# A graph kernel's node pass shared over three spread stages instead of two, and one DVE step moved

## The chip, the core and the metric

The kernel runs on one core of one Trainium2 chip. The core has five engines that take their own instruction streams and meet at semaphores: PE (TensorE, matrix products; its weight loads are shown apart as PEld), DVE (VectorE), ACT (ScalarE), POOL (GpSimd; here it issues the gathers) and SP (SyncE; here it issues the plain DMAs). The metric is the device time of one execution in microseconds (us), as the median of several runs. A lower time is better.

## The reference, cut to what matters

50,000 nodes with 64 features (N, D), 25,000 edges sorted by destination. Two layers, each on a layer norm with a ReLU: four GAT attention layers in a row, and one crystal-graph convolution. Cut:

```
h  = relu(layernorm(x))
for i in range(4):                              # L = 4 attention layers
    fs    = (h @ Ws[i]).reshape(N, 4, 64)
    e     = leaky_relu(el[src] + er[dst])
    alpha = softmax of e over the edges of one destination (self loops too)
    h     = segment_sum(alpha * fs[src], dst).sum(heads) + bias
x1 = x + h + h_bias                             # "x1": every node, all 50,000
h  = relu(layernorm(x1))
t  = batch_norm(concat(h[src], h[dst], edge_attr) @ W_full)
x  = x1 + softplus(h + batch_norm(segment_sum(sigmoid(t1) * softplus(t2), dst)))
```

Most nodes are no destination of any edge. For those the four attention layers reduce to one fixed 64x64 product on relu(layernorm(x)). The kernel computes that product for all nodes in a **node pass** (98 groups of 512 nodes), which needs nothing of the attention layers, and writes rows of x1 to a table; rows for destinations come from the edge side.

## The kernel before

Edges are padded to 196 tiles of 128, taken as G = 49 groups of 4 tiles (512 edges). Each attention layer l is a row of stages with barriers between them: softmax_weights (some 20 us), messages(l), and for l = 0, 1, 2 spread(l). The semaphores of a layer are cleared behind its stages. After the last layer come the convolution, its batch norms and the output.

**spread(l)** carries the sums of a destination back along its edges and fetches each edge's source row. It has 49 edge groups. What is done per edge group k, by engine:

- POOL: four indirect gathers (L930), 4 buffers of groups deep: it waits for the scan of group k-4 and else runs freely.
- SP: a load of the mask row keep_next (L940).
- PE: weights (L974), one 64x512 product, and dst_side (L981), four 128x72 products.
- DVE: end, the masking (ended, L1015), back, a reversed scan (h_new, L1022) that follows the scan of the group before, and combine (L1030 to L1032), which needs the gathered rows of the group and dst_side.
- ACT: finish, a copy of the scan into wide (L1079).

In spread(0) and spread(1) (`with_nodes = l < 2`) the same loop also carries one node group per edge group, 49 in each, so that all 98 are done; spread(2) has none. The node work of a group:

- SP: load_nodes (L946), and save_nodes, two stores (L952, L954). The load waits for x1_ready of the group four back.
- DVE: n_sum L1036, n_center L1041, n_variance L1046, n_normalize L1051, n_finish L1057 (adds nodes to bank 5, writes x1_out, raises x1_ready).
- ACT: n_squares L1084, n_scales L1088 and L1090, n_take L1095 (copies the transposes out).
- PE: n_transposes (L989), n_outs (L996), four 128x64 products into bank 5. n_outs waits for n_take of its group and x1_ready of the group before, since bank 5 is one buffer.

The order on each engine is written by hand: `pipelined(eng, stages)` runs i = 0 to 52 and, in each turn i, calls every (lag, fn) of the list with k = i - lag, if 0 <= k < 49. So the list's order is the engine's order within a turn. A **turn** below is one i. Before, DVE's list is normalize(3), end(1), back(1), combine(3), variance(2), sum(1), center(1), finish(4), the lag in brackets; PE's is outs(4), weights(0), transposes(3), dst_side(2).

Of the kernel before, what the change touches and what calls it, by code (L numbers as in the profile page):

```python
# [28 lines left out]
P = 128  # L29
D = 64  # L30
H = 4
L = 4
# [6 lines left out]
G = TILES // TPG  # L39
# [7 lines left out]
NODE_T2 = 4  # L47
GN2 = NODE_T2 * P
# [4 lines left out]
AHEAD = 4  # L53
# [38 lines left out]
def build(nc, x, src, dst, edge_attr, Ws, attn_l, attn_r, gat_bias, h_bias, W_full, b_full,  # L92
# [5 lines left out]
    LAST_P2 = (N - (2 * G - 1) * GN2) // NODE_T2  # L98
# [17 lines left out]
    def mem(stack, name, shape, dt=F32):  # L116
        return stack.enter_context(nc.sbuf_tensor(name, shape, dt))
# [3 lines left out]
    def sem(stack, name):  # L121
        signals.append(nc.alloc_semaphore(name=name))
        return signals[-1]
# [17 lines left out]
    with top:  # L141
# [742 lines left out]
        def spread(l):  # L884
# [2 lines left out]

            with ExitStack() as st:
                SLOTS = 4
                uses = [(G - s + SLOTS - 1) // SLOTS for s in range(SLOTS)]  # L890
                with_nodes = l < 2
                if with_nodes:
                    nodes = mem(st, f"nodes_{l}", [P, SLOTS, NODE_T2, D])
                    x1_out = mem(st, f"x1_out_{l}", [P, 2, NODE_T2, 2 * D])
                    n_norm = mem(st, f"n_norm_{l}", [P, SLOTS, NODE_T2, D + 1])
                    n_square = mem(st, f"n_square_{l}", [P, NODE_T2, D])
                    n_norm_t = mem(st, f"n_norm_t_{l}", [D + 1, GN2])
                    n_stat = mem(st, f"n_stat_{l}", [P, SLOTS, 3, NODE_T2])
                    n_logs = mem(st, f"n_logs_{l}", [P, NODE_T2])
                    nodes_in = [sem(st, f"nodes_in_{l}_{s}") for s in range(SLOTS)]  # L900
                    x1_saved = [sem(st, f"x1_saved_{l}_{s}") for s in range(2)]
                    ones_set = sem(st, f"ones_set_{l}")
                    n_summed, n_centered, n_squared, n_summed2, n_logged, n_rstd, n_normed, n_in_psum, n_t_ready, n_out, x1_ready = [
                        sem(st, f"n_{name}_{l}") for name in ("summed", "centered", "squared", "summed2", "logged", "rstd", "normed",
                                                             "in_psum", "t_ready", "out", "x1_ready")]
# [29 lines left out]
                @block.sync  # L935
                def _(sp):
                    def load(k, g, s, turn):
                        sp.wait_ge(spread_out, at(k, back=2))
                        sp.sem_inc(sp_paced, 1)
                        sp.dma_start(keep[:, s % 2], lanes(keep_row[bass.ds(g * GE + 1, GE)], D)).then_inc(keep_in[s], 16)  # L940

                    def load_nodes(k, g, s, turn):
                        used = LAST_P2 if isinstance(k, int) and k == G - 1 and l == 1 else P
                        sp.wait_ge(x1_ready, at(k, back=4))
                        sp.sem_inc(sp_paced, 1)
                        sp.dma_start(nodes[0:used, s], x[bass.ds((k + l * G) * GN2, used * NODE_T2)].rearrange("(p j) f -> p j f", j=NODE_T2)).then_inc(nodes_in[s], 16)  # L946

                    def save_nodes(k, g, s, turn):
                        used = LAST_P2 if isinstance(k, int) and k == G - 1 and l == 1 else P
                        sp.wait_ge(x1_ready, at(k))  # L950
                        sp.sem_inc(sp_paced, 1)
                        sp.dma_start(tables[L - 1][bass.ds((k + l * G) * GN2, used * NODE_T2)].rearrange("(p j) f -> p j f", j=NODE_T2),  # L952
                                     x1_out[0:used, s % 2, :, 0:D]).then_inc(x1_saved[s % 2], 16)
                        sp.dma_start(node_rows[bass.ds((k + l * G) * GN2, used * NODE_T2)].rearrange("(p j) f -> p j f", j=NODE_T2),  # L954
                                     x1_out[0:used, s % 2]).then_inc(x1_saved[s % 2], 16)

                    if with_nodes:
                        sp.wait_ge(ones_set, 3)
                        for s in range(2):
                            sp.sem_inc(x1_saved[s], 16)  # L960
                        pipelined(sp, ((0, load), (4, save_nodes), (0, load_nodes)), down=True, slots=SLOTS)
                        for s in range(2):
                            sp.wait_ge(x1_saved[s], 32 * (uses[s] + uses[s + 2]) + 16)
                    else:
                        pipelined(sp, ((0, load),), down=True, slots=SLOTS)

                @block.tensor
                def _(t_):
# [30 lines left out]
                    if with_nodes:  # L999
                        for signal in (n_in_psum, n_out):  # L1000
                            t_.sem_inc(signal, AHEAD)
                        pipelined(t_, ((4, n_outs), (0, weights), (3, n_transposes), (2, dst_side)), down=True, slots=SLOTS)
                    else:
                        pipelined(t_, ((0, weights), (2, dst_side)), down=True, slots=SLOTS)

                @block.vector
                def _(v):
# [51 lines left out]
                    if with_nodes:  # L1059
                        for signal in (n_summed, n_centered, n_summed2, n_normed, x1_ready):  # L1060
                            v.sem_inc(signal, AHEAD)
                        v.memset(n_norm[:], 1.0).then_inc(ones_set, 1)
                        v.memset(nodes[:], 0.0).then_inc(ones_set, 1)
                        v.memset(x1_out[:, :, :, D:2 * D], 0.0).then_inc(ones_set, 1)
                        v.wait_ge(ones_set, 3)
                        pipelined(v, ((3, n_normalize), (1, end), (1, back), (3, combine), (2, n_variance), (1, n_sum), (1, n_center),
                                      (4, n_finish)), down=True, slots=SLOTS)
                    else:
                        pipelined(v, ((1, end), (1, back), (3, combine)), down=True, slots=SLOTS)

                @block.scalar
                def _(s_):
# [24 lines left out]
                    if with_nodes:  # L1097
                        for signal in (n_squared, n_logged, n_rstd, n_t_ready):
                            s_.sem_inc(signal, AHEAD)
                        pipelined(s_, ((1, finish), (3, n_take), (2, n_scales), (1, n_squares)), down=True, slots=SLOTS)  # L1100
                    else:
                        pipelined(s_, ((1, finish),), down=True, slots=SLOTS)

        def attention_step(l):
            with ExitStack() as st:
# [675 lines left out]
```

## Time and profile before

| | us |
|---|---|
| median of 3 runs | 3240.72 |
| lowest, highest run | 3231.77, 3241.5 |
| the profiled execution, its own time | 3232.58 |
| its span, first to last instruction | 3230.8 |
| mean granted TensorE clock over the span | 0.818 of 2.4 GHz |

Busy over the span: PE 2319.8 us (72%), DVE 2235.8 (69%), POOL 1427.3 (44%), ACT 1248.5 (39%). No engine is the bound of the whole; each stage has a limit of its own. The three spreads are found in the timeline by POOL's gathers of L930: spread(0) begins at 818 us, spread(1) at 1341, spread(2) at 1869; each ends where DVE's first step of the next softmax (L649) starts.

A timeline row reads: start us, duration us, engine, line, operation, output <- input, count, and in brackets the engine's idle time ahead of it and what released it.

### The profile page before, as it was taken

To read this page: it belongs to the slowest core of one execution; us is meant where nothing else is said; L and a number is where in the kernel's file an instruction comes from. 1 tells how busy PE (TensorE), PEld (TensorE's weight loads), DVE (VectorE), ACT (ScalarE), POOL (GpSimd) and SP (SyncE) were. 2 spreads that over 40 slices of the span, in tenths; PEclk is the share of its full clock that TensorE was granted. 3 is DMA by queue.
4 is the path that set the end of the run, shared out by engine and by line. 5 is a ranking of instruction groups with operands and counts; after the bars stand their busy time and mean duration, and the time that the engine had idled before them with its cause. 6 is when DMAs were issued, how large, how long until landed. Compare 5 with 4: busy or idle time off the path is not lost. (4 is left out here: it accounts for less than half of the span.)

```text
span 3230.8 us, 38240 instructions
## 1 busy us (share of the span) xinstructions
PE 2319.8 (72%) x10796; PEld 1499.2 (46%) x10796; DVE 2235.8 (69%) x3888; ACT 1248.5 (39%) x2599; POOL 1427.3 (44%) x1389
## 2 busy tenths in 40 slices
PE   1998888399788689889859977739977772110575
PEld 1766665255565445466635533325533331000565
DVE  4766664677777677677767744458889986664698
ACT  0333323244333234333324411114445556663587
POOL 5777774000677200377500067720057763777000
PEclk9999999999767689866759965559989985555898
DMA  2333332011444301255411111102233321222464
GB/s 60 105 108 99 94 100 78 15 46 46 101 124 123 85 32 46 62 124 125 118 30 47 46 37 34 34 13 79 78 74 72 72 63 30 63 71 67 138 202 139
DMA packets 310382, 248.80 MB, mean 77 GB/s; under 512 B 149840, under 2 KB 258639, under 8 KB 310154
## 3 DMA queue, kind: packets, MB, share of 16 engines
q1 hardware_dynamic: 266270, 197.56, 20.1%
q0 software_dynamic: 43904, 48.80, 8.3%
q8 instruction: 90, 1.47, 0.2%
q14 instruction: 118, 0.97, 0.1%
HBM read 125.76 MB, written 118.06 MB: 75 GB/s over the span
## 5 line engine op out<-in xcount | busy, mean ns | idle before, releaser
L930 POOL DMA_INDIRECT edge<-table,row_of_source x588 | 589.3, 1002 | 963.6 <-POOLq L753 778.8
L871 PE MATMUL banks<-scaled_t,w_heads 128*64 128x512 f32 x784 | 380.3, 607 | 0.0
L815 DVE TENSOR_TENSOR_SCAN wide<-keep,wide,banks 64x512 f32<-64x512 uint8 x196 | 249.5, 1273 | 187.4 <-issue 162.6
L1238 POOL DMA_INDIRECT edge<-table,row_of_x x196 | 227.3, 1160 | 303.4 <-POOLq L131 242.2
L981 PEld LDWEIGHTS banks<-w_edge_full,wide 128*128 128x128 f32 x1176 | 219.9, 279 | 146.6 <-issue 139.5
L849 ACT ACTIVATE ring<-wide 128x512 f32<-128x512 f32 x196 | 123.6, 630 | 425.1 <-DVE wide L815 425.1
L981 PE MATMUL banks<-w_edge_full,wide 128*128 128x72 f32 x1176 | 227.5, 360 | 70.5 <-DVE self_logit L1032 69.7
L1497 POOL DMA_INDIRECT node_rows<-rows_conv,scatter_row x196 | 218.9, 1117 | 118.3 <-ACT rows_conv L1535 68.0
L878 PEld LDWEIGHTS banks<-w_row,ring 128*128 128x128 f32 x1568 | 189.7, 191 | 160.9 <-issue 149.3
L974 PE MATMUL banks<-wide,w_row 128*64 128x512 f32 x294 | 250.6, 953 | 16.2 <-DVEq L1009 9.9
L1079 ACT ACTIVATE wide<-h_new 64x512 f32<-64x512 f32 x147 | 92.6, 630 | 435.4 <-DVE h_new L1022 435.4
L808 DVE TENSOR_TENSOR scaled<-edge,alpha 128x1024 f32<-128x1024 f32 x196 | 236.7, 1209 | 3.7 <-PE banks L863 3.7
L190 POOL DMA_INDIRECT edge<-in_x_dram,src_row x196 | 194.2, 991 | 81.4 <-issue 57.9
L190 POOL DMA_INDIRECT got<-in_x_dram,dst_row x196 | 194.4, 992 | 59.7 <-issue 59.1
L878 PE MATMUL banks<-w_row,ring 128*128 128x68 f32 (+1 forms) x1568 | 217.1, 281 | 4.6 <-ACT ring L849 4.6
L863 PE MATMUL banks<-ident,scaled 128*128 128x128 f32 x1568 | 210.3, 279 | 11.4 <-DVE scaled L808 11.4
L1611 PE MATMUL banks<-ident,last_sum 64*128 64x64 f32 x196 | 32.3, 318 | 247.8 <-ACT rows_conv L1535 192.6
L587 PE MATMUL banks<-w_chain,norm_t 64*128 64x204 f32 x392 | 204.8, 625 | 2.5 <-ACT self_logit L565 2.5
L996 PE MATMUL banks<-w_node,n_norm_t 65*128 65x64 f32 x784 | 144.8, 346 | 73.5 <-DVE x_out L1057 69.5
L863 PEld LDWEIGHTS banks<-ident,scaled 128*128 128x128 f32 x1568 | 184.1, 150 | 16.3 <-DVE scaled L808 12.8
L1022 DVE TENSOR_TENSOR_SCAN h_new<-keep_next,h_new,ended 64x512 f32<-64x512 uint8 x147 | 187.9, 1278 | 5.2
L996 PEld LDWEIGHTS banks<-w_node,n_norm_t 65*128 65x128 f32 x784 | 134.1, 257 | 80.5 <-issue 64.9
(300 smaller groups left out, 4530.6 us busy)
## 6 DMA issues: line engine op xcount, KB each, us to landing
node_rows<-x_out SPq DMA_DIRECT2D x97, 256.0 KB
wide<-node_rows SPq DMA_DIRECT2D x48, 512.0 KB, 3.6
table<-chain_rows SPq DMA_DIRECT2D x147, 136.0 KB, 2.2
table<-rows SPq DMA_DIRECT2D x147, 136.0 KB, 2.3
nodes<-in_x_dram SPq DMA_DIRECT2D x97, 128.0 KB, 2.9
table<-x_out SPq DMA_DIRECT2D x97, 128.0 KB
out_dram<-n_soft SPq DMA_DIRECT2D x48, 256.0 KB, 2.1
sources<-src_pad SPq DMA_DIRECT2D x49, 196.0 KB
```

The costliest lines, as they stand in the source:

```text
L190: pool.indirect_dma_start(out=to, out_offset=None, in_=x, in_offset=bass.IndirectOffsetOnAxis(ap=rows[:, tile:tile + 1], axis=0),).then_in ...
L808: v.tensor_tensor(scaled[:, s], edge[:, tiles, 0:D].unsqueeze(2).broadcast_to([P, TPG, H, D]), inner(alpha[:, tiles], [P, TPG, H, D]), ALU ...
L815: v.tensor_tensor_scan(out=wide[0:D, bass.ds(g * GE + 1, GE)], data0=keep[:, s], data1=bank[2 + s][0:D], initial=wide[0:D, bass.ds(g * GE, ...
L863: last = t_.transpose(bank[6 * s + pair][:, t * P:(t + 1) * P], scaled[:, s, t, 2 * pair:2 * pair + 2].rearrange("p h f -> p (h f)"), iden ...
L871: last = t_.matmul(bank[2 + s][0:D], w_heads[:, l, pair], scaled_t[:, s, pair], start=pair == 0, stop=pair == 1)
L878: last = t_.matmul(bank[4 + s][:, t * width:(t + 1) * width], ring[:, s, t * P:(t + 1) * P], w_row[:, l, 0:width], start=True, stop=True)
L930: pool.indirect_dma_start(out=edge[:, at_tile], out_offset=None, in_=tables[l], in_offset=bass.IndirectOffsetOnAxis(ap=row_of_source[:, at ...
L974: t_.matmul(bank[s % 2][0:D], w_row[:, l, 0:D], wide[:, bass.ds(g * GE + 1, GE)], start=True, stop=True).then_inc(through, 1)
L981: last = t_.matmul(bank[2 + s % 2][:, t * EDGE_W:(t + 1) * EDGE_W], here, w_edge_full[:, l + 1], start=True, stop=True)
L996: last = t_.matmul(bank[5][:, j * D:(j + 1) * D], n_norm_t[:, j * P:(j + 1) * P], w_node[:], start=True, stop=True)
L1238: pool.indirect_dma_start(out=edge[:, tile, 0:D], out_offset=None, in_=tables[l], in_offset=bass.IndirectOffsetOnAxis(ap=row_of_x1[:, tile ...
L1497: pool.indirect_dma_start(out=node_rows, out_offset=bass.IndirectOffsetOnAxis(ap=scatter_row[:, tile:tile + 1], axis=0), in_=rows[:, s, t] ...
```

## The change

The 98 node groups are shared over the three spreads: 32, 33 and 33 (2·49·l // 3 is the first). The node stages of a spread are called only for k < 32 or 33, through a wrapper `some`; the edge groups stay 49 in each. spread(2) now has the node buffers, semaphores, three memsets and the end's wait on the stores that the other two had. On DVE, n_finish moves from the end of a turn to behind end, ahead of back.

```diff
-                with_nodes = l < 2
-                if with_nodes:
-                    nodes = mem(st, f"nodes_{l}", [P, SLOTS, NODE_T2, D])
+                first_group = 2 * G * l // (L - 1)
+                groups = 2 * G * (l + 1) // (L - 1) - first_group
+
+                def some(fn):
+                    return lambda k, g, s, turn: fn(k, g, s, turn) if k < groups else None
+
+                nodes = mem(st, f"nodes_{l}", [P, SLOTS, NODE_T2, D])
...
-                        sp.dma_start(nodes[0:used, s], x[bass.ds((k + l * G) * GN2, used * NODE_T2)].rearrange("(p j) f -> p j f", j=NODE_T2)).then_inc(nodes_in[s], 16)
+                        sp.dma_start(nodes[0:used, s], x[bass.ds((k + first_group) * GN2, used * NODE_T2)].rearrange("(p j) f -> p j f", j=NODE_T2)).then_inc(nodes_in[s], 16)
...
+                    pipelined(sp, ((0, load), (4, some(save_nodes)), (0, some(load_nodes))), down=True, slots=SLOTS)
+                    for s in range(2):
+                        sp.wait_ge(x1_saved[s], 32 * ((groups - s + 1) // 2) + 16)
...
-                        pipelined(t_, ((4, n_outs), (0, weights), (3, n_transposes), (2, dst_side)), down=True, slots=SLOTS)
-                    else:
-                        pipelined(t_, ((0, weights), (2, dst_side)), down=True, slots=SLOTS)
+                    pipelined(t_, ((4, some(n_outs)), (0, weights), (3, some(n_transposes)), (2, dst_side)), down=True, slots=SLOTS)
...
-                        pipelined(v, ((3, n_normalize), (1, end), (1, back), (3, combine), (2, n_variance), (1, n_sum), (1, n_center),
-                                      (4, n_finish)), down=True, slots=SLOTS)
-                    else:
-                        pipelined(v, ((1, end), (1, back), (3, combine)), down=True, slots=SLOTS)
+                    pipelined(v, ((3, some(n_normalize)), (1, end), (4, some(n_finish)), (1, back), (3, combine), (2, some(n_variance)),
+                                  (1, some(n_sum)), (1, some(n_center))), down=True, slots=SLOTS)
...
-                        pipelined(s_, ((1, finish), (3, n_take), (2, n_scales), (1, n_squares)), down=True, slots=SLOTS)
-                    else:
-                        pipelined(s_, ((1, finish),), down=True, slots=SLOTS)
+                    pipelined(s_, ((1, finish), (3, some(n_take)), (2, some(n_scales)), (1, some(n_squares))), down=True, slots=SLOTS)
```

DVE in spread(0), one turn in the run of full turns. Before:

```order
L1051 SCALAR_TENSOR_TENSOR n_norm_0<-n_norm_0,n_stat_0 128x4x64
L1015 SCALAR_TENSOR_TENSOR ended_0<-keep_next_0,banks 64x512
L1022 SCALAR_TENSOR_TENSOR h_new_0<-keep_next_0,h_new_0,ended_0 64x512
L1030 TENSOR_TENSOR edge<-edge,banks 128x4x64
L1031 TENSOR_TENSOR edge<-edge,banks 128x4x4
L1032 TENSOR_SCALAR self_logit<-banks 128x16
L1046 TENSOR_REDUCE n_stat_0<-n_square_0 128x4
L1036 TENSOR_REDUCE n_stat_0<-nodes_0 128x4
L1041 SCALAR_TENSOR_TENSOR n_norm_0<-n_stat_0,nodes_0 128x4x64
L1057 TENSOR_TENSOR x1_out_0<-banks,nodes_0 128x4x64
```

The change, the last turn that still has n_normalize, the last with n_finish, and the first with neither (lines are three or so less, since the code above them is shorter):

```order
L1048 SCALAR_TENSOR_TENSOR n_norm_0<-n_norm_0,n_stat_0 128x4x64
L1012 SCALAR_TENSOR_TENSOR ended_0<-keep_next_0,banks 64x512
L1054 TENSOR_TENSOR x1_out_0<-banks,nodes_0 128x4x64
L1019 SCALAR_TENSOR_TENSOR h_new_0<-keep_next_0,h_new_0,ended_0 64x512
L1027 TENSOR_TENSOR edge<-edge,banks 128x4x64
L1028 TENSOR_TENSOR edge<-edge,banks 128x4x4
L1029 TENSOR_SCALAR self_logit<-banks 128x16
L1012 SCALAR_TENSOR_TENSOR ended_0<-keep_next_0,banks 64x512
L1054 TENSOR_TENSOR x1_out_0<-banks,nodes_0 128x4x64
L1019 SCALAR_TENSOR_TENSOR h_new_0<-keep_next_0,h_new_0,ended_0 64x512
```

The step x1_out now stands between ended and the scan h_new, and after it only the edge steps are left.

PE in spread(0) where the node groups stop. Before, at the same place, the four kinds go on to the stage's end:

```order
L974 MATMUL banks<-wide,w_row 64x512
L989 MATMUL banks<-ident,n_norm_0 65x128 x4
L981 MATMUL banks<-w_edge_full,wide 128x72 x4
L996 MATMUL banks<-w_node,n_norm_t_0 128x64 x4
L974 MATMUL banks<-wide,w_row 64x512
L989 MATMUL banks<-ident,n_norm_0 65x128 x4
```

The change:

```order
L981 MATMUL banks<-w_edge_full,wide 128x72 x4
L996 MATMUL banks<-w_node,n_norm_t_0 128x64 x4
L974 MATMUL banks<-wide,w_row 64x512
L981 MATMUL banks<-w_edge_full,wide 128x72 x4
L974 MATMUL banks<-wide,w_row 64x512
L981 MATMUL banks<-w_edge_full,wide 128x72 x4
```

The last turns of the stage hold weights and dst_side alone, as all turns of spread(2) did before.

## Rows read from the trace of the kernel before

**Rows 1.** Windows, the three spreads: stretch, length, busy and instructions by engine, clock, DMA.

```profile
818.00:1105.00 287.00, 242.47 (x1078) 170.93 (x1078) 209.67 (x493) 97.80 (x246) 200.60 (x196) 0.71 0.48 118
1341.00:1630.00 289.00, 252.43 (x1078) 178.68 (x1078) 209.27 (x492) 96.83 (x246) 195.49 (x196) 0.68 0.48 118
1868.00:2124.00 256.00, 177.27 (x490) 95.95 (x490) 120.21 (x246) 32.13 (x50) 193.26 (x196) 0.55 0.19 33
```

**Rows 2.** Groups by line, POOL alone, spread(0), (1), (2): busy, mean ns, idle before.

```profile
L930 POOL DMA_INDIRECT edge<-table,row_of_source x196 | 200.6, 1023 | 309.2 <-POOLq L753 249.8 <-issue 59.4
...
L930 POOL DMA_INDIRECT edge<-table,row_of_source x196 | 195.5, 997 | 328.8 <-POOLq L753 262.9 <-issue 57.6 <-DVE h_new L1022 8.3
...
L930 POOL DMA_INDIRECT edge<-table,row_of_source x196 | 193.3, 986 | 325.6 <-POOLq L753 266.2 <-issue 59.4
```

**Rows 3.** Timeline: first gather of each spread, last combine, first step behind it.

```profile
818.21 0.94 POOL L930 DMA_INDIRECT edge<-table,row_of_source  x1 [249.77 <-POOLq L753]
...
1112.56 0.97 DVE L649 TENSOR_TENSOR edge<-edge,const_logit 128x784 f32<-128x784 f32 x1 [7.50 <-PEq L131]
...
1341.13 0.94 POOL L930 DMA_INDIRECT edge<-table,row_of_source  x1 [262.89 <-POOLq L753]
...
1638.54 0.98 DVE L649 TENSOR_TENSOR edge<-edge,const_logit 128x784 f32<-128x784 f32 x1 [8.11 <-PEq L131]
...
1868.66 0.94 POOL L930 DMA_INDIRECT edge<-table,row_of_source  x1 [266.15 <-POOLq L753]
...
2122.88 0.42 DVE L1030 TENSOR_TENSOR edge<-edge,banks 128x256 f32<-128x256 f32 x1 [4.38 <-DMA edge<-table,row_of_source]
...
2131.80 0.97 DVE L649 TENSOR_TENSOR edge<-edge,const_logit 128x784 f32<-128x784 f32 x1 [8.33 <-PEq L131]
```

**Rows 4.** Timeline, POOL: the first gather of edge group k = 32 in each spread.

```profile
986.87 0.94 POOL L930 DMA_INDIRECT edge<-table,row_of_source  x1 [0.30 <-issue]
...
1507.74 1.35 POOL L930 DMA_INDIRECT edge<-table,row_of_source  x1 [0.31 <-issue]
...
2034.35 0.94 POOL L930 DMA_INDIRECT edge<-table,row_of_source  x1 [0.31 <-issue]
```

**Rows 5.** Timeline, DVE in spread(0): the scans of groups 3, 32 and 48.

```profile
835.24 1.28 DVE L1022 TENSOR_TENSOR_SCAN h_new<-keep_next,h_new,ended 64x512 f32<-64x512 uint8 x1
...
1000.26 1.28 DVE L1022 TENSOR_TENSOR_SCAN h_new<-keep_next,h_new,ended 64x512 f32<-64x512 uint8 x1
...
1090.84 1.28 DVE L1022 TENSOR_TENSOR_SCAN h_new<-keep_next,h_new,ended 64x512 f32<-64x512 uint8 x1
```

**Rows 6.** Timeline, PE in spread(1): one turn at the low clock.

```profile
1489.66 1.90 PE L996 MATMUL banks<-w_node,n_norm_t 65*128 65x64 f32 x8
1491.50 1.97 PE L974 MATMUL banks<-wide,w_row 128*64 128x512 f32 x2
1493.39 1.12 PE L989 MATMUL banks<-ident,n_norm 128*65 128x128 f32 x4
1494.31 1.82 PE L981 MATMUL banks<-w_edge_full,wide 128*128 128x72 f32 x8
1495.92 1.47 PE L996 MATMUL banks<-w_node,n_norm_t 65*128 65x64 f32 x6
```

**Rows 7.** Timeline in spread(0), a turn at the full clock: scan, ACT's copy, n_take.

```profile
1069.48 1.27 DVE L1022 TENSOR_TENSOR_SCAN h_new<-keep_next,h_new,ended 64x512 f32<-64x512 uint8 x1
...
1070.88 0.63 ACT L1079 ACTIVATE wide<-h_new 64x512 f32<-64x512 f32 x1 [1.92 <-DVE h_new L1022]
...
1071.53 0.59 ACT L1095 ACTIVATE n_norm_t<-banks 65x512 f32<-65x512 f32 x1
```

**Rows 8.** Waits in spread(0): engine and line, released by, us in total, times, longest.

```profile
DVE n_stat L1036 <- DMA nodes<-in_x_dram: 48.8, 41, 2.3
```

**Rows 9.** Timeline, DVE at the start of spread(2): scans of groups 0 and 3.

```profile
1871.34 1.28 DVE L1022 TENSOR_TENSOR_SCAN h_new<-keep_next,h_new,ended 64x512 f32<-64x512 uint8 x1
...
1878.19 1.28 DVE L1022 TENSOR_TENSOR_SCAN h_new<-keep_next,h_new,ended 64x512 f32<-64x512 uint8 x1
```

More of the change, by code:

```diff
@@ new lines, in spread @@
+                n_norm_t = mem(st, f"n_norm_t_{l}", [D + 1, GN2])
+                n_stat = mem(st, f"n_stat_{l}", [P, SLOTS, 3, NODE_T2])
+                n_logs = mem(st, f"n_logs_{l}", [P, NODE_T2])
+                nodes_in = [sem(st, f"nodes_in_{l}_{s}") for s in range(SLOTS)]
+                x1_saved = [sem(st, f"x1_saved_{l}_{s}") for s in range(2)]
+                ones_set = sem(st, f"ones_set_{l}")
+                n_summed, n_centered, n_squared, n_summed2, n_logged, n_rstd, n_normed, n_in_psum, n_t_ready, n_out, x1_ready = [
+                    sem(st, f"n_{name}_{l}") for name in ("summed", "centered", "squared", "summed2", "logged", "rstd", "normed",
+                                                         "in_psum", "t_ready", "out", "x1_ready")]
@@ L953, in save_nodes @@
                                      x1_out[0:used, s % 2, :, 0:D]).then_inc(x1_saved[s % 2], 16)
-                        sp.dma_start(node_rows[bass.ds((k + l * G) * GN2, used * NODE_T2)].rearrange("(p j) f -> p j f", j=NODE_T2),
+                        sp.dma_start(node_rows[bass.ds((k + first_group) * GN2, used * NODE_T2)].rearrange("(p j) f -> p j f", j=NODE_T2),
                                      x1_out[0:used, s % 2]).then_inc(x1_saved[s % 2], 16)
[L957 to L963, printed above, removed]
-                    else:
-                        pipelined(sp, ((0, load),), down=True, slots=SLOTS)
+                    sp.wait_ge(ones_set, 3)
@@ L967, in _ @@
+                    for s in range(2):
+                        sp.sem_inc(x1_saved[s], 16)
+                    pipelined(sp, ((0, load), (4, some(save_nodes)), (0, some(load_nodes))), down=True, slots=SLOTS)
+                    for s in range(2):
+                        sp.wait_ge(x1_saved[s], 32 * ((groups - s + 1) // 2) + 16)
                 @block.tensor
@@ L997, in n_outs @@
                         last.then_inc(n_out, 1)
-                    if with_nodes:
-                        for signal in (n_in_psum, n_out):
-                            t_.sem_inc(signal, AHEAD)
-                        pipelined(t_, ((4, n_outs), (0, weights), (3, n_transposes), (2, dst_side)), down=True, slots=SLOTS)
-                    else:
-                        pipelined(t_, ((0, weights), (2, dst_side)), down=True, slots=SLOTS)
+                    for signal in (n_in_psum, n_out):
+                        t_.sem_inc(signal, AHEAD)
+                    pipelined(t_, ((4, some(n_outs)), (0, weights), (3, some(n_transposes)), (2, dst_side)), down=True, slots=SLOTS)
                 @block.vector
@@ L1057, in n_finish @@
                         v.tensor_tensor(x1_out[:, s % 2, :, 0:D], bank[5][:, 0:NODE_T2 * D].rearrange("p (j f) -> p j f", f=D), nodes[:, s], ALU.add).then_inc(x1_ready, 1)
[L1059 to L1065, printed above, removed]
[L1066 to L1069 removed]
+                    for signal in (n_summed, n_centered, n_summed2, n_normed, x1_ready):
+                        v.sem_inc(signal, AHEAD)
+                    v.memset(n_norm[:], 1.0).then_inc(ones_set, 1)
+                    v.memset(nodes[:], 0.0).then_inc(ones_set, 1)
+                    v.memset(x1_out[:, :, :, D:2 * D], 0.0).then_inc(ones_set, 1)
+                    v.wait_ge(ones_set, 3)
+                    pipelined(v, ((3, some(n_normalize)), (1, end), (4, some(n_finish)), (1, back), (3, combine), (2, some(n_variance)),
+                                  (1, some(n_sum)), (1, some(n_center))), down=True, slots=SLOTS)
                 @block.scalar
```

28 lines of the change are left out of this document (8 added, 20 removed).

## The prediction

> **What bounds the kernel now.** The change touches only the three spreads, so I read the windows of those stretches first. The two with nodes keep PE and DVE well filled over 287 and 289 us; the one without has PE at 177 and DVE at 120 of 256 us [rows 1]. POOL's busy time is nearly the same in all three, 200.6, 195.5 and 193.3 us [rows 2]. The second view is POOL's group by line: its idle time inside a stage is 0.3 us between gathers ("issue", 59.4 us) and, in spread(1) only, 8.3 us behind the scan. So its gathers take 260.0, 261.4 and 252.7 us from first start to last end.
>
> The third view is the timeline at the stages' edges [rows 3]. From the first gather to the first step of the next softmax it is 1112.56 - 818.21 = 294.35 us, 1638.54 - 1341.13 = 297.41 us, and 2131.80 - 1868.66 = 263.14 us: 854.9 us in all. In spread(2) POOL sets the end: its last combine waits for the gather, 1.5 us after POOL's last end (1868.66 + 252.7 = 2121.4, combine at 2122.88), and the softmax starts 10.45 us behind POOL's end. In spread(0) POOL is done 34 us ahead of the stage's end, at 1078.2: there PE and DVE are last. Their pace is (1090.84 - 835.24) / 45 = 5.68 us a turn [rows 5], while POOL's is 260.0 / 49 = 5.31. The gap of some 0.4 us a turn piles up over 49 turns, and a tail of node turns stands behind it.
>
> What makes 5.68: the granted clock in spread(0) is 0.71, a mixture of 1.2 and 2.4 GHz [rows 1]. A turn at the low clock is 6.26 us (1495.92 - 1489.66), of which PE is busy all through [rows 6]: n_outs 1.84, weights 1.89, transposes 0.92, dst_side 1.61, start to start. At the full clock it is shorter and DVE waits for the nodes' load, 48.8 us in spread(0) [rows 8], since the load waits for n_finish at the end of a turn.
>
> **The change part by part.** *Edge groups without nodes.* 17 groups of spread(0) and 16 each of spread(1) and (2) now have none. Such a turn at the low clock costs PE 1.89 + 1.61 = 3.50 us. At the start of spread(2), at the full clock, three turns took 1878.19 - 1871.34 = 6.85, or 2.28 each [rows 9]. POOL wants 5.1 to 5.3. So behind the last node group PE and DVE gain 1.6 us or more a turn on POOL. Do they catch up? I take the worst mixture that the rows show: the old pace as far as group 32, then the low clock throughout. Scan 32 stands at 1000.26 - 818.21 = 182.1 us after the first gather. Two more full turns and one without transposes: 182.1 + 12.5 + 5.3 = 199.9 for scan 35. Thirteen turns of 3.50: 245.4 for scan 48; two more turns and the scan's 1.3: combine 48 could start at 253.7. POOL lets it start at some 255.7 + 1.5 = 257.2 (next step). POOL ends last, by 3.5 us, and by more with any turn at the full clock. What is late next in all three spreads is thus POOL.
>
> *POOL's own time.* It slows a little beside node work. Its first 32 groups took 986.87 - 818.21 = 168.7 us in spread(0), 1507.74 - 1341.13 = 166.6 in spread(1) and 2034.35 - 1868.66 = 165.7 in spread(2), where no nodes were [rows 3, 4]. The remaining 17 groups, without nodes, took 2121.4 - 2034.35 = 87.0. I add 87.0 to each node part: 255.7, 253.6, and for spread(2) the mean of the two node parts, 167.6 + 87.0 = 254.6. POOL also waits for the scan four groups back: group 39 would start near 205, scan 35 ends at 201.2 even in the slow case above, and from there scans run ahead. No term for that.
>
> *The end of a stage.* 10.45 us from POOL's end to the next softmax, as in spread(2). Its stores, formerly behind the last node group, are then long done.
>
> *spread(2)* gets three memsets (they stood ahead of the first turn in the other two, beside POOL's first gathers), the node loads and stores on SP's queue, and more semaphores to clear. Memsets and queue are hidden: POOL waits for nothing of them in its first four groups, and DVE then has the slack above. The clearing does not show in rows; spread(0), with its node semaphores, took 7.50 us behind DVE's last step where spread(2) took 8.33 [rows 3]. I take 0; the ends are 0 and 1 us.
>
> *n_finish behind the masking.* Per turn 0 instructions more. It lets the load start some 3 us earlier (scan, combine, variance, sum, center stood before it) and so should remove most of the 48.8 us of rows 8 at the full clock, and PE's next n_outs comes free earlier. In exchange the scan waits for n_out. The loop that this closes is scan start to ACT's copy 1.40, copy to n_take 0.65, n_take 0.59 [rows 7], n_outs 1.84 at the low clock [rows 6], n_finish 0.42 (its neighbours' length): 4.90 us, below the 6.26 of PE. So no turn gets longer, and turns at the full clock may get down towards POOL's 5.2. Under POOL that is slack: worth 0 in the sum.
>
> **Sum.** Spread(0): 255.7 + 10.45 = 266.1, from 294.35: -28.2. Spread(1): 253.6 + 10.45 = 264.1, from 297.41: -33.3. Spread(2): 254.6 + 10.45 = 265.1, from 263.14: +2.0. Together -59.5 us on the profiled execution's own 3232.58, hence 3173. That execution lies near the lowest of the runs; the three runs and it have a mean of 3236.6. From there: 3177. I give **3177**.
> Bounds of the unknown terms: POOL as quick in all as in spread(2), 3 x 263.14 = 789.4, is -65.5; POOL at spread(0)'s 260.0 over all 49 groups, and 1 us of clearing, is 3 x 270.5 + 1 = 812.3, or -42.6. With the runs' own 3231.8 to 3241.5 that is 3166 to 3199.
>
> **On the clock, the Trainium skill.** The low clock's rows are PE-bound turns; spread(2), whose PE had least work, was granted 0.55 [rows 1]. The Trainium skill says in "TensorE: Matmul & The Clock Gate", section "What's actually happening", that the half-rate state is the default and PE's activity lifts it. By this rule the thinned turns and, in balance with POOL, the node turns would go at the lower rate; the rows of spread(2) agree for the thinned ones.
>
> **Rivals.**
> 1. *PE stays at the low clock through the node turns* as well, because it is no longer behind and so pauses. For it: 0.55 in spread(2) [rows 1]. Against it: at 6.26 PE has no pause, and this very state gave way to the full clock time and again in spreads (0) and (1). Time: scan 3 at 17.0, scan 32 at 17.0 + 29 x 6.26 = 198.6, scan 35 at 216.4, scan 48 at 261.9, combine 48 at 270.2, the softmax 8.9 after it: 279.1 for each spread, 837.3 in all, -17.6 us, so 3219.
> 2. *Slower than before: n_finish's wait holds the scan in a longer loop.* One place: DVE between masking and scan. If PE, in its fixed order, put weights (1.97) between n_take and n_outs, the loop would be 4.90 + 1.97 = 6.87 us a turn at the low clock. A spread is 17.0 + 31 p + 5.3 + 45.5 + 8.3 + 8.9 for a turn of p; it passes 285.0 (854.9 / 3) from p = 6.45. At 6.87 it is 298.0, 894 in all, +39 us, so 3276. Against it: PE's order has n_outs first, and the loop has 1.36 us to spare.
> 3. *The change doesn't do what it says*: spreads (0) and (1) stay as long because the thinned turns don't catch up. If they ran at POOL's 5.16 from scan 35 on: 199.9 + 15 x 5.16 + 1.3 + 8.9 = 287.5 in each, 862.5, +8 us: 3244. Against it: 2.28 a turn in rows 9, and nothing in a thinned turn waits for more than its own gather.
>
> **How the numbers follow.** POOL-bound spreads, my forecast: 0.83. Rival 1 or something between it and the forecast: 0.10. Rival 2: 0.03. Rival 3: 0.04, split evenly between no change and slower. The range takes the forecast's bounds and reaches a little towards rival 1: **3162 to 3205**. A measurement of this kernel tells apart about 0.3%, some 10 us. Faster by more than that: 0.93. Within: 0.02. Slower: 0.05.
>
> **What would show it.** Right: in every spread the last combine waits for the gather's DMA, as in spread(2) before, and the first gather to the softmax is 263 to 268 us three times; POOL has no wait behind the scan; scan 48 of spread(0) stands near 245 after the first gather or earlier, not 273. The wait of n_sum for the nodes' load falls clearly. PE's clock is lower behind group 33 than before it. Wrong: a last combine that waits for dst_side or the scan; POOL waits behind h_new in tens of us; waits at n_finish for n_outs near 1 us in most turns, with turns over 6.3; a gather mean well above 1023 ns; or messages stages that change their length, which the sum takes as fixed.

## The result, and the profile after

The changed kernel takes **3187.18 us** (median of 4 runs, 3185.08 to 3191.02) beside 3236.24 us for the kernel before (4 runs, 3229.4 to 3241.5). The ratio is 0.985, 95% interval [0.983, 0.987]: 1.5% faster, some 49 us. The forecast was 3177, from 3162 to 3205. Its direction and its range held; the gain was 10 to 15 us smaller than the sum.

The profiled execution took 3188.4 us (span 3186.6). The windows of its three spreads answer to [rows 1]; the columns are the same:

```profile
818.00:1077.00 259.00, 223.54 (x874) 149.42 (x874) 176.43 (x407) 74.44 (x178) 197.29 (x196) 0.63 0.43 98
1316.00:1576.00 260.00, 212.75 (x886) 142.15 (x886) 177.75 (x411) 75.62 (x182) 199.83 (x196) 0.67 0.43 100
1816.00:2076.00 260.00, 215.62 (x886) 142.56 (x886) 177.77 (x410) 76.05 (x182) 199.81 (x196) 0.66 0.43 99
```

The three are alike now, PE at 213 to 224 us and DVE at 176 to 178. POOL by line in the same three stretches, as in [rows 2]:

```profile
L933 POOL DMA_INDIRECT edge<-table,row_of_source x196 | 197.3, 1007 | 308.9 <-POOLq L753 249.5 <-issue 59.1 <-DVE h_new L1019 0.3
...
L933 POOL DMA_INDIRECT edge<-table,row_of_source x196 | 199.8, 1020 | 300.5 <-POOLq L753 241.1 <-issue 59.1 <-DVE h_new L1019 0.3
...
L933 POOL DMA_INDIRECT edge<-table,row_of_source x196 | 199.8, 1019 | 300.0 <-POOLq L753 240.6 <-issue 59.4
```

And the edges of the stages, as in [rows 3]. The first row is spread(0)'s last combine (its first gather starts at 818.55):

```profile
1076.76 0.42 DVE L1027 TENSOR_TENSOR edge<-edge,banks 128x256 f32<-128x256 f32 x1 [4.38 <-DMA edge<-table,row_of_source]
...
1086.69 0.97 DVE L649 TENSOR_TENSOR edge<-edge,const_logit 128x784 f32<-128x784 f32 x1 [9.35 <-PEq L131]
...
1316.36 0.94 POOL L933 DMA_INDIRECT edge<-table,row_of_source  x1 [241.10 <-POOLq L753]
...
1587.04 0.98 DVE L649 TENSOR_TENSOR edge<-edge,const_logit 128x784 f32<-128x784 f32 x1 [9.29 <-PEq L131]
...
1816.19 0.94 POOL L933 DMA_INDIRECT edge<-table,row_of_source  x1 [240.58 <-POOLq L753]
...
2086.85 0.98 DVE L649 TENSOR_TENSOR edge<-edge,const_logit 128x784 f32<-128x784 f32 x1 [9.29 <-PEq L131]
```

The last combine waits 4.38 us for its gather (4.33 and 4.34 in the other two spreads): POOL sets the end, as forecast. First gather to next softmax is 268.14, 270.68 and 270.66 us, 809.5 in all, where 854.9 stood: **-45.4 us**. The rest of the kernel is the same within noise: 229 to 230 us from each softmax to the next spread in both traces, and 1091.9 and 1092.7 us from the last one to the end of the last instruction that counts as busy. That gives a clean measure, used for all experiments below: the **sum of the three spreads** in the profiled execution. It is free of the tail behind the layers, which alone moved between 1083 and 1093 us over the runs.

### The profile page after: what moved, and what is told of

It is laid out like the page before. It is cut to its first block and busy times, and to the rows that moved or that the text cites. A ratio compares the mean times of both kernels' runs of the same rounds, so it can differ in the third digit from the quotient of the medians.

```text
span 3186.6 us, 38276 instructions
## 1 busy us (share of the span) xinstructions
PE 2305.1 (72%) x10796; PEld 1490.8 (47%) x10796; DVE 2230.3 (70%) x3891; ACT 1248.8 (39%) x2599; POOL 1434.1 (45%) x1389
## 5 line engine op out<-in xcount | busy, mean ns | idle before, releaser
L933 POOL DMA_INDIRECT edge<-table,row_of_source x588 | 596.9, 1015 | 909.4 <-POOLq L753 731.2
L974 PE MATMUL banks<-wide,w_row 128*64 128x512 f32 x294 | 241.6, 920 | 19.4 <-DVEq L1006 10.1
L863 PEld LDWEIGHTS banks<-ident,scaled 128*128 128x128 f32 x1568 | 184.0, 150 | 16.7 <-DVE scaled L808 13.3
L996 PE MATMUL banks<-w_node,n_norm_t 65*128 65x64 f32 x784 | 136.9, 332 | 37.7 <-ACT n_norm_t L1089 37.7
L871 PEld LDWEIGHTS banks<-scaled_t,w_heads 128*64 128x64 f32 x784 | 91.7, 137 | 148.6 <-issue 148.3
```

The lines of the kernel that those rows point to most:

```text
L863: last = t_.transpose(bank[6 * s + pair][:, t * P:(t + 1) * P], scaled[:, s, t, 2 * pair:2 * pair + 2].rearrange("p h f -> p (h f)"), iden ...
L871: last = t_.matmul(bank[2 + s][0:D], w_heads[:, l, pair], scaled_t[:, s, pair], start=pair == 0, stop=pair == 1)
L933: pool.indirect_dma_start(out=edge[:, at_tile], out_offset=None, in_=tables[l], in_offset=bass.IndirectOffsetOnAxis(ap=row_of_source[:, at ...
L974: t_.matmul(bank[s % 2][0:D], w_row[:, l, 0:D], wide[:, bass.ds(g * GE + 1, GE)], start=True, stop=True).then_inc(through, 1)
```

## Experiments

The measured sums in one table. "Busy" is POOL's in the 588 gathers of the spreads. A median stands where there were four runs.

| kernel | spreads, us | sum | POOL busy | total |
|---|---|---|---|---|
| before | 294.4, 297.4, 263.1 | 854.9 | 589.3 | 3236.2 |
| changed | 268.1, 270.7, 270.7 | 809.5 | 596.9 | 3187.2 |
| e1 share only | 271.7, 271.2, 266.8 | 809.6 | 591.5 | 3182.4 |
| e2 n_finish only | 277.8, 273.6, 264.4 | 815.8 | 601.9 | 3187.6 |
| e3 more load | 269.3, 271.5, 275.6 | 816.4 | 602.8 | 3195.7 (1 run) |
| e4 more DVE | 275.7, 277.3, 276.1 | 829.2 | 616.6 | 3205.0 (1 run) |
| e5 more reduce | 277.1, 276.7, 273.9 | 827.8 | 615.2 | 3196.6 (1 run) |
| e6 normalize on ACT | 271.2, 271.2, 266.4 | 808.8 | 596.2 | 3183.5 |
| e7 split clear | 266.5, 270.8, 270.2 | 807.4 | 600.0 | 3178.4 |
| e8 more semaphores | 269.2, 273.9, 271.5 | 814.6 | 598.1 | 3189.7 (1 run) |
| e9 scan from PSUM | 257.2, 257.6, 257.2 | 772.0 | 559.3 | 3146.8 |
| e10 e9 with more DVE | 258.0, 257.4, 257.7 | 773.1 | 560.5 | 3146.3 (1 run) |
| e11 all together | 255.1, 255.4, 255.3 | 765.7 | 558.0 | 3139.0 |

### The two parts apart

e1 is the changed kernel with DVE's old order:

```diff
-pipelined(v, ((3, some(n_normalize)), (1, end), (4, some(n_finish)), (1, back), (3, combine), ..., (1, some(n_center))), ...)
+pipelined(v, ((3, some(n_normalize)), (1, end), (1, back), (3, combine), ..., (1, some(n_center)), (4, some(n_finish))), ...)
```

> The 32/33/33 sharing alone; DVE's n_finish stays at the end of its turn, as before. Theory A (POOL sets all three spreads as soon as the last 16 turns carry no nodes; moving n_finish only makes slack): the node turns go at the old 5.7 us, group 32's scan stands near 182 us after the first gather, but the tail catches up, the last combine of each spread waits for its gather, each spread is 266 to 271 us, the total within 5 us of the changed kernel's 3187. Rival B (the move of n_finish is what keeps PE and DVE level with POOL): the last combine waits for PE or DVE, spreads of 275 us or more, total 3205 or more.

Measured: 3182.36 us (3179.59 to 3184.22), ratio 0.984 [0.982, 0.986]. The node turns went at 5.87, 5.85 and 5.70 us, scan 32 stood 187.4 us after the first gather of spread(0), and n_sum waited as before:

```profile
DVE n_stat L1033 <- DMA nodes<-in_x_dram: 39.6, 28, 2.4
```

All the same scan 48 stood at 248.0, the last combine at 261.9 behind its gather, and the spreads sum to 809.6. Theory A held: the thinned turns do catch up, from a worse start than the forecast assumed. They took 2.4 us each between scans 38 and 42. The equal sum is made up differently: POOL was busy 5.4 us less than in the changed kernel, and in spread(0) it waited 7.1 us behind the scan. By the totals e1 is 4.8 us the quicker; its tail behind the layers, which neither edit touches, is 5.9 us shorter (1086.8 against 1092.7).

e2 is the kernel before with n_finish moved:

```diff
-pipelined(v, ((3, n_normalize), (1, end), (1, back), (3, combine), (2, n_variance), (1, n_sum), (1, n_center), (4, n_finish)), ...)
+pipelined(v, ((3, n_normalize), (1, end), (4, n_finish), (1, back), (3, combine), (2, n_variance), (1, n_sum), (1, n_center)), ...)
```

> n_finish moved ahead of the scan, node groups still 49, 49 and none. Theory A: the move alone quickens a node turn from 5.7 to at most POOL's pace of 5.2 to 5.3, so the first two spreads lose some 15 us each of the 34 us that stood behind POOL's end, and keep the tail of four node turns: total near 3205 to 3215. Rival B (at the low clock PE bounds the turn, so the move changes little): turns stay above 5.5 us, total 3228 or more.

Measured: 3187.59 us (3182.54 to 3191.88), ratio 0.986 [0.984, 0.988]: more than theory A gave it, and nearly the whole gain of the two together. As far as scan 32 the node turns went at 5.14 and 5.07 us, and over scans 3 to 48 at 5.34 and 5.17, where before it was 5.68 and 5.74. POOL ends 264.5 and 261.7 us after its first gather, and only the tail stands behind it. DVE in spread(0)'s last turns:

```profile
1081.17 0.42 DVE L1057 TENSOR_TENSOR x_out<-banks,nodes 128x256 f32<-128x256 f32 x1 [1.18 <-PE banks L996]
...
1085.33 0.42 DVE L1057 TENSOR_TENSOR x_out<-banks,nodes 128x256 f32<-128x256 f32 x1 [1.83 <-PE banks L996]
...
1088.84 0.42 DVE L1057 TENSOR_TENSOR x_out<-banks,nodes 128x256 f32<-128x256 f32 x1 [2.59 <-PE banks L996]
```

So the two parts are two ways to the same bound. The move took away the wait of n_sum for its load, 48.8 us in spread(0) before and 0.0 here. Between scans 3 and 32, the turns that saw both levels of the clock fell from 5.86 and 5.62 us to 4.97 and 5.05, those at the low level alone only from 5.98 and 6.19 to 5.84 and 5.90. The granted clock over the two stretches was 0.71 and 0.73, near the 0.71 and 0.68 of before, so the gain is not one of the clock alone. The sharing on top of it takes 6.3 us off the sum: 5.0 of POOL's own time from first gather to last end (780.2 to 775.2) and 1.3 of the stages' ends. Three kernels that treat POOL alike (the changed one, e7 and e8) differ by 3 us in the first of these, and by the totals, whose ranges overlap, the gain cannot be told.

### What slows POOL's gathers

The forecast's largest miss is POOL's own time: 256.7, 259.2 and 259.2 us where it had 255.7, 253.6 and 254.6. I tried traffic against DVE.

e3 issues each node group's load twice, into a spare buffer:

```diff
+                        sp.dma_start(idle_in[0:used, s], x[... same rows ...]).then_inc(idle_sem[s], 16)
```

> The changed kernel with each node group's load issued a second time by SP, into a buffer that nobody reads (128 KB more per group, same engines' work). POOL's gathers took 199.8 us in the later spreads, against 193.3 beside no nodes. Theory C (the gathers are slowed by the DMA traffic beside them): long gathers grow in number, POOL's busy time in each spread rises by 3 us or more. Rival D (they are slowed by DVE's work): POOL's busy time stays within 1.5 us of 197.3, 199.8 and 199.8.

Measured: busy 602.8 us, +5.9 over three spreads; by spread 198.2, 200.1 and 204.5, so that only the last exceeds what runs differ by. Theory C wanted 3 us in each: not borne out. The count of the held gathers below settles it.

e4 repeats n_center's step twice into a scratch:

```diff
+                        for m in range(2):
+                            v.scalar_tensor_tensor(out=idle_out[:, m], in0=inner(n_stat[:, s, 0], [P, NODE_T2, D]), scalar=-1.0 / D,
+                                                   in1=nodes[:, s], op0=ALU.mult, op1=ALU.add)
```

> The changed kernel with n_center's instruction issued twice more per node group, into a buffer that nobody reads (0.85 us more of DVE per turn, no DMA more). Rival D (DVE's work slows the gathers): POOL's busy time in each spread rises by 2 us or more. Theory C (traffic slows them): POOL's busy time stays within 1.5 us. If turns now fall behind POOL, they are caught up in the thinned turns and the spreads stay near 268 to 271 us; the total within 6 us of the changed kernel.

Measured: busy 616.6 us, +19.7, sum of the spreads 829.2, again +19.7, with POOL last in all three. D held, but the total was 18 us over the changed kernel and not within 6. I took it for a price per step, 0.10 us for each instruction with two SBUF operands, and tested that from both sides.

e5 repeats n_sum's reduction instead, one operand from SBUF:

```diff
+                        for m in range(2):
+                            v.tensor_reduce(idle_out[:, m], nodes[:, s], AX_X, ALU.add)
```

> The changed kernel with n_sum's reduction issued twice more per node group into a scratch that nobody reads: 0.8 us more of DVE per turn, as in the run with two more n_center steps, but each reads one operand from SBUF where n_center reads two. That run's gathers took 616.6 us over the three spreads against 596.9. Theory P (a DVE instruction with two SBUF operands holds up a gather): POOL's busy time stays within 4 us of 596.9 and the three spreads sum to 805 to 815 us. Rival Q (any DVE time beside it does, or turns that are simply too full): POOL's busy time is 608 or more, or the spreads sum to 822 or more.

Measured: busy 615.2 us, sum 827.8. Theory P falls as the only cause: nearly the same cost with one operand.

e6 takes n_normalize off DVE:

```diff
+                    def n_normalize(k, g, s, turn):      # on ACT
+                        s_.wait_ge(n_rstd, at(k))
+                        for j in range(NODE_T2):
+                            part = n_norm[:, s, j, 0:D]
+                            last = s_.activation(part, part, ACT.Relu, scale=n_stat[:, s, 2, j:j + 1])
+                        last.then_inc(n_normed, 1)
```

> The changed kernel with n_normalize moved from DVE (one step with two SBUF operands, 98 in all) to ACT (four Relu activations of 64 columns with the reciprocal deviation as scale). Theory P: 196 such steps added cost 19.7 us of POOL's busy time, 0.10 each, so 98 removed give back about 10: POOL's busy time near 587, the spreads sum to about 799, total near 3177. Rival Q' (ACT's four instructions delay n_take and with it PE, or the gathers are not affected): POOL's busy time within 3 us of 597 or turns fall behind; total 3184 or more.

Measured: 3183.52 us, busy 596.2: nothing given back. Neither a price per step alone nor plain DVE time explains that; what was left is where DVE's work puts something. The trace of e5 shows what; POOL, the scan (L1020) and ACT's copy behind it (L1076), in order of time:

```profile
867.02 1.09 POOL L934 DMA_INDIRECT edge<-table,row_of_source  x1 [0.30 <-issue]
868.14 1.27 DVE L1020 TENSOR_TENSOR_SCAN h_new<-keep_next,h_new,ended 64x512 f32<-64x512 uint8 x1
868.42 1.74 POOL L934 DMA_INDIRECT edge<-table,row_of_source  x1 [0.30 <-issue]
869.53 0.63 ACT L1076 ACTIVATE wide<-h_new 64x512 f32<-64x512 f32 x1 [2.71 <-DVE h_new L1020]
870.47 0.94 POOL L934 DMA_INDIRECT edge<-table,row_of_source  x1 [0.30 <-issue]
871.72 1.09 POOL L934 DMA_INDIRECT edge<-table,row_of_source  x1 [0.30 <-issue]
872.83 1.27 DVE L1020 TENSOR_TENSOR_SCAN h_new<-keep_next,h_new,ended 64x512 f32<-64x512 uint8 x1
873.11 1.75 POOL L934 DMA_INDIRECT edge<-table,row_of_source  x1 [0.30 <-issue]
```

The gather at 868.42 starts 0.28 us into the scan and ends at 870.16, 0.75 us behind the scan's end at 869.41; turn after turn it falls in the same place. Of the gathers over 1.2 us in the spreads all end in this way, 43 of 43 before, 61 of 61 after the change, 70 of 70 in e5. An undisturbed one takes 0.94. That instant is also the end of ACT's copy, which follows the scan by 0.12 us and takes 0.63, so ACT could have been the holder too.

e9 leaves ACT as it is and changes what the scan reads. The masked values go back into their PSUM bank, and PE's next product into that bank waits for the scan:

```diff
-                        t_.wait_ge(ended_ready, at(k, back=2))
+                        t_.wait_ge(spread_out, at(k, back=2))
-                        v.scalar_tensor_tensor(out=ended[:, s % 2], in0=keep[:, s % 2], scalar=0.0, in1=bank[s % 2][0:D],
+                        v.scalar_tensor_tensor(out=bank[s % 2][0:D], in0=keep[:, s % 2], scalar=0.0, in1=bank[s % 2][0:D],
-                        v.tensor_tensor_scan(out=h_new[:, s % 2, ::-1], data0=keep[:, s % 2, ::-1], data1=ended[:, s % 2, ::-1],
+                        v.tensor_tensor_scan(out=h_new[:, s % 2, ::-1], data0=keep[:, s % 2, ::-1], data1=bank[s % 2][0:D, ::-1],
```

> The changed kernel; in the spreads the masked values go back into their PSUM bank instead of an SBUF buffer, so that the scan behind them reads one operand from SBUF and one from PSUM (PE's next product into that bank waits for the scan). In the traces so far every gather over 1.2 us ends 0.75 us behind the end of a scan, and the longest are as long as a scan and that together. Theory R (the scan, with both operands in SBUF, holds the gather whose start falls into it; where in a gather it falls is fixed by the DVE work between a gather's landing and the scan): no gathers above 1.2 us in the spreads, POOL's busy time falls from 596.9 to near 588 x 0.95 = 559, the spreads sum to 768 to 780 us, total near 3150. Rival U (the scan holds gathers whatever it reads, or its place is chance): busy time stays within 5 us of 597 and the total within 5 us of 3187.

Measured: **3146.78 us** (3140.34 to 3152.82), ratio 0.975 [0.972, 0.977]. POOL's group by line over the whole kernel, and a gather that starts inside a scan:

```profile
L933 POOL DMA_INDIRECT edge<-table,row_of_source x588 | 559.3, 951 | 910.3 <-POOLq L753 731.9 <-issue 174.7 <-DVE h_new L1019 3.7
```

```profile
904.30 1.26 DVE L1019 TENSOR_TENSOR_SCAN h_new<-keep_next,h_new,banks 64x512 f32<-64x512 uint8 x1
904.53 0.94 POOL L933 DMA_INDIRECT edge<-table,row_of_source  x1 [0.31 <-issue]
905.68 0.63 ACT L1073 ACTIVATE wide<-h_new 64x512 f32<-64x512 f32 x1 [3.71 <-DVE h_new L1019]
```

It starts 0.23 us into the scan, with ACT's copy behind it as ever, and takes 0.94. No gather is over 1.2 us. Theory R held in all its numbers, and ACT is cleared. The Trainium skill says in "SBUF — State Buffer", section "Who interferes with whom", that a DVE instruction with two SBUF inputs contends with a GpSimd instruction that reads SBUF. For the scan the trace agrees: 37.6 us of POOL's busy time went with one of its two operands.

e10 puts e4's steps on top of e9:

> The kernel of the run before this one with n_center's step issued twice more per node group, as in the run that cost 19.7 us of POOL's busy time when the scan read SBUF alone. Theory R: the extra steps only moved the scan's place in a gather, which now costs nothing; POOL's busy time stays within 4 us of the run before this one. Theory P (each step with two SBUF operands holds a gather by itself): busy time rises by 10 to 20 us. In both the node turns may fall behind POOL's 5.0 us and be caught up in the thinned ones.

Measured: busy 560.5 us, sum 773.1, total 3146.3 in one run, against 559.3, 772.0 and 3146.8. The steps that cost 19.7 us before cost 1.1. They have two SBUF operands too (0.42 us each, a value broadcast along a row and the nodes), and it looks as if they held nothing. The rows say otherwise. A gather of e10 that starts inside such a step:

```profile
1895.55 0.42 DVE L1052 SCALAR_TENSOR_TENSOR n_norm<-n_norm,n_stat 128x256 f32<-128x256 f32 x1
1895.58 1.21 POOL L934 DMA_INDIRECT edge<-table,row_of_source  x1 [0.30 <-issue]
```

It ends at 1896.79, 0.82 us behind the step's end at 1895.97. A gather that nothing holds takes 0.94, so a step of 0.42 us can add no more than some 0.3 us to one, where a scan adds up to 1.0. I count the gathers of the spreads that took more than 0.965 us, and what they took beyond 0.945, by what they start inside:

| kernel | scan: us beyond | n_center, its repeats, n_normalize: us beyond | POOL busy |
|---|---|---|---|
| before | 29.9 | 4.3 | 589.3 |
| changed | 39.8 | 2.0 | 596.9 |
| e3 more load | 45.0 | 2.7 | 602.8 |
| e4 more DVE | 49.9 | 11.5 | 616.6 |
| e5 more reduce | 53.6 | 6.5 | 615.2 |
| e9 scan from PSUM | 0 | 3.1 | 559.3 |
| e10 e9 with more DVE | 0 | 5.4 | 560.5 |

What is left of POOL's busy time is 555 to 556 us in every row. The held gathers start inside a scan with two SBUF operands, or inside one of the short steps with two; in all fourteen traces the first end 0.75 to 0.77 us behind it and the second 0.81 to 0.83. In the changed kernel 153 gathers start inside a scan and 93 of them are held. Of the other 60, 53 start in its last 0.22 us and 7 in its first 0.1. None is held of the 97 that start inside the masking (0.67 us, one operand from PSUM) or the 74 that start inside a reduction. So theory P was half right: of e4's 19.7 us, 10.1 are longer holds by the scan and 9.5 holds by the short steps, which e10's expectation had put at nothing. And the doubled load of e3 lengthened no gather that starts outside these steps; why more of them fell into a scan there is open.

### The exit of a stage

From the last combine to the softmax it is 9.9 us in the changed kernel (1086.69 - 1076.76), and was 8.9 in the old spread(2). e8 adds 18 semaphores to each spread, e7 deals the clearing out over five engines:

```diff
+            for part, on in enumerate((block.sync, block.scalar, block.vector, block.tensor, block.gpsimd)):
+                on(clear(part))          # each clears signals[part::5]
```

> The changed kernel with 18 more semaphores per spread, which nobody uses and SP clears. Theory S: each of the three exits grows by 1.0 us, from 9.9 to 10.9. Rival T: they stay at 9.9.

> The changed kernel; the clearing of the semaphores behind each layer (and the other stages that do it) is dealt out over the five engines, where SP alone cleared them. From the last combine to the next softmax it is 9.9 us in all three spreads now, and was 8.9 in the old spread(2), which had 18 semaphores fewer. Theory S (SP's clearing stands on the path, about 0.055 us each): four fifths of some 60 a layer go off it, the three exits shrink to near 7.5 us, total 3175 to 3180. Rival T (the extra us is something else, such as the barrier): exits stay at 9.9, total within 4 us of 3187.

Measured from POOL's last end to the softmax: 12.42, 12.92 and 12.89 us in e8, 9.75, 9.74 and 9.59 in e7, against 11.43, 11.44 and 11.44. Its first step in each, changed kernel, e8, e7 (L652 in the last):

```profile
1086.69 0.97 DVE L649 TENSOR_TENSOR edge<-edge,const_logit 128x784 f32<-128x784 f32 x1 [9.35 <-PEq L131]
```

```profile
1088.44 0.97 DVE L649 TENSOR_TENSOR edge<-edge,const_logit 128x784 f32<-128x784 f32 x1 [10.30 <-PEq L131]
```

```profile
1085.28 0.97 DVE L652 TENSOR_TENSOR edge<-edge,const_logit 128x784 f32<-128x784 f32 x1 [7.62 <-PEq L131]
```

The idle time in the brackets is the reading: 9.35, 10.30, 7.62. Theory S held: SP's clearing is on the path, 1.0 to 1.5 us for 18 semaphores (0.05 to 0.08 each). Splitting it gave 1.7 us a stage, less than the 2.4 expected. e7's total is 3178.37 (3173.0 to 3185.67) and overlaps the changed kernel's.

### All together

e11 has e9's change in the spreads and in the convolution's first stage, and e7's clearing.

> The same scan operand in PSUM in the spreads and also in the convolution's first stage, whose 196 gathers took 1155 ns in the mean (226 us busy), and the clearing of semaphores dealt out over five engines. Theory R: the convolution's gathers fall to near 950 ns as well, but that stage is as long as DVE makes it (turns of some 5.3 us there beside 5.8 for POOL), so that it gives 10 to 25 us; with 5 to 9 us of the clearing the total is 3115 to 3140. Rival U: within 5 us of the split-clearing run's 3178.

Measured: **3139.0 us** (3131.75 to 3142.73), ratio 0.971 [0.969, 0.973], the fastest of the study. The convolution's gathers in e9 and in e11, from section 5 of the page:

```profile
L1229 POOL DMA_INDIRECT edge<-table,row_of_x x196 | 226.6, 1156 | 305.6 <-POOLq L131 244.4
```

```profile
L1232 POOL DMA_INDIRECT edge<-table,row_of_x x196 | 189.2, 965 | 314.5 <-POOLq L131 241.9
```

The hold went there too, 1156 to 965 ns, and POOL's last gather of the stage starts 261 us after the first where it was 287. But the scans there run over 277.2 us in e11 and 276.1 in e9, first start to last end: DVE and PE set that stage, and it gave nothing. The 7.8 us between e9 and e11 are about the clearing (6.3 us of the spreads' sum). So the part of the expectation that gave the convolution 10 to 25 us was wrong, though it had named the reason.

### The kernel before with the scan from PSUM

> The kernel before (node groups 49, 49 and none, n_finish at the end of its turn) with the masked values in PSUM as the scan's operand. Theory R with A: its spread(2), where POOL is last, shortens from 263.1 to about 257 us; its first two spreads, where PE and DVE are last, stay within 5 us of 294 and 297, though their gathers get quicker too (busy near 187 against 200.6 and 195.5). Total near 3226. Rival V (a quicker POOL helps wherever it runs): the first two spreads shorten by 10 us or more each, total under 3210.

Measured: 3596.1 us, with 3584.8 us for the kernel before beside it, one run each. Both kernels took 11% longer here than in all other runs, so the times cannot be held against the others. The gathers alone can be read: busy 557.4 us and none over 1.2 us. That the total gained nothing beside its companion speaks for theory R, but a single pair in such a run settles nothing, and the sums of its spreads are not comparable. It stays open.

## Why the prediction was right, and where it was off

- **POOL sets all three spreads: right.** The last combine waits 4.38 us for its gather, and POOL waited 0.6 us in all behind scans. Scan 48 stood at 244.4 us in spread(0), where "near 245 or earlier" was named. e1 shows the step that carries this, the catching up, by itself, and at 2.4 us a turn between scans 38 and 42, near the 2.28 read from [rows 9] (which were granted 0.88, not quite the full clock) and not at the 3.50 of the worst case.
- **n_finish's move worth 0 in the sum: right beside the sharing** (809.6 without it, 809.5 with it). Its effect on the turns was as described: node turns 5.25, 5.13 and 5.13 us, n_sum's wait gone, 0.0 in the lines of spread(0). What the text did not see is that the move alone is worth 39 us of the same 45 (e2). The sum was right for the change as a whole and silent on its parts: either part alone brings nearly all of it, so neither can be credited with it.
- **POOL's own time: mis-sized.** The forecast carried the node part's old slowdown over and took 763.9 us in all; it was 775.1, 11.2 more, inside the bounds given. Some 8 us of it lie in the first 32 groups (169.4, 169.9 and 171.8 us where it had 168.7, 166.6 and 167.6) and 3 in the last 17 (87.3, 89.3 and 87.5 where it had 87.0). "It slows a little beside node work" names only a part of the cause: spread(2) before, without nodes, had 8.3 us of holds by its scans too, beside 13.1 and 8.5 by the scans and 2.4 and 1.9 by the short steps in the other two. The holder is shown, by e9, e10 and the count of held gathers. That the old node part had run beside turns of 5.7 us, and that turns in step with POOL put more scans on a gather, is argued from these, not shown by itself.
- **The stage's end: mis-sized by 1.0 us each.** "I take 0" for the clearing was wrong; its bound of 1 us for one stage should have been one for three, since 10.45 was read from the spread with the fewest semaphores. e7 and e8 show it.
- **Sum.** -59.5, plus 11.2, plus 3.0: -45.3, measured -45.4 in the spreads and -44.2 in the profiled executions. The two mis-sized terms also took the spreads past the "263 to 268 us three times" that was named as a sign of being right: they are 268.1, 270.7 and 270.7.
- **The clock.** Behind the node groups the granted clock fell to 0.50, 0.57 and 0.50; it had stood at 0.68 to 0.72 ahead of them. The Trainium skill says in "TensorE: Matmul & The Clock Gate", section "What's actually happening", that the half rate is the default and activity lifts it; the direction agrees. But thinned turns are not slow by themselves: in e1, where they had to catch up, it was 0.98 to 1.00 in the stretches with scans 35 to 44, and 0.50 to 0.60 once POOL set the pace. Rival 1 took the low clock too far: the node turns kept their mixture.
- **Rivals 2 and 3: not seen.** DVE waits for n_outs ahead of the scan in half the node turns of spread(0), 16.7 us in all, 1.0 us each. A few turns grew: five of the 87 between scans 3 and 32 took over 6.3 us, the longest 7.51, where before it was three of 58 and 6.69. The mean fell all the same, to 5.25, 5.13 and 5.13.

```profile
DVE edge L1027 <- DMA edge<-table,row_of_source: 43.8, 18, 4.4
DVE x_out L1054 <- PE banks L996: 16.7, 16, 2.6
```

## What to carry to other kernels

Where two engines are last in a stage and a third stands just behind, any of several edits brings the same gain, down to the third engine's time: measure the parts apart before crediting one. Then look at the third engine's instructions one by one: those that are longer than the shortest show, by what they start inside and end with, who holds them. Take all of them and not the longest alone: a short holder makes only slightly long ones. And time that is freed on an engine which is not last in its stage, as in the convolution, is worth nothing until that changes.

## What the runs showed of the hardware

- A gather that starts inside a DVE scan with both operands in SBUF ends 0.75 us behind the scan, up to 1.93 us long where it takes 0.94. Of the 153 that start in a scan of the changed kernel, 60 are not held: 53 in its last 0.22 us, 7 in its first 0.1. With one of the operands in PSUM none is held, and the scan is no slower (1.26 us).
- A step of 0.42 us with two SBUF operands holds a gather as well, to 0.82 us behind the step's end, up to 1.21 us long. It costs little because it is short: 5.4 us in all in e10, with three such steps per node group besides n_normalize.
- Doubling the nodes' loads (e3) left the gathers that start outside these DVE steps at 0.94 us.
- SP's clearing of semaphores behind a stage costs 0.05 to 0.08 us for each, on the path.
